# A gated delta-rule recurrence: a chunk's output made by GpSimd, the running products in two parts, the gate's products placed one step later

## What is computed

```python
def step(S, inp):                      # S: 64 x 64 per batch and head, 4 x 16 of them
    qt, kt, vt, at, bt = inp
    err = jnp.einsum('bhij,bhj->bhi', S, kt) - vt
    S = at[..., None] * S - bt[..., None, None] * (err[..., None] * kt[:, :, None, :])
    o = jnp.einsum('bhij,bhj->bhi', S, qt)
    return (S, o)
...
_, o = lax.scan(step, S0, xs)          # 1024 steps
...
mu = o.mean(-1, keepdims=True)
var = ((o - mu) ** 2).mean(-1, keepdims=True)
o = (o - mu) / jnp.sqrt(var + EPS) * ln_w + ln_b
g = jax.nn.sigmoid(x @ Wg.T).reshape(Bb, Tt, H, DV)
o = (o * g).reshape(Bb, Tt, H * DV)
return o @ Wo.T
```

## Time and profile before

| | us |
|---|---|
| median of 3 runs | 4159.57 (4156.91 to 4163.24) |
| the profiled execution's time | 4161.57 |
| its span | 4159.6 |
| DVE busy in the span | 3381.1 (81%) |
| PE busy | 3273.8 (79%) |
| POOL busy | 2340.0 (56%) |
| ACT busy | 2225.8 (54%) |
| L1050 and L1056, 960 instructions each | 723.3 and 723.0 |
| L819, 768 instructions | 552.0 |

### The profile page before, as it was taken

The page is one execution under the profiler, slowest core; times in us unless marked ns, Lnnn a source line. Parts: engine busy times, 40 slices in busy tenths (PEclk is TensorE's granted clock), DMA queues, the critical chain, the costliest instruction groups (busy, mean ns, idle before and its releaser), DMA issues. The chain is left out here.

```text
span 4159.6 us, 113184 instructions
## 1 busy us (share of the span) xinstructions
PE 3273.8 (79%) x45929; PEld 2775.5 (67%) x45929; DVE 3381.1 (81%) x6208; ACT 2225.8 (54%) x5291; POOL 2340.0 (56%) x3045
## 2 busy tenths in 40 slices
PE   5778778777777777777777774377999979988998
PEld 3677777777777777777777774354666647755775
DVE  4599999999999999999999998206888868856885
ACT  3444444444444444444444442324888779936982
POOL 0476776776776767767767766332000058806870
PEclk9888888888888988888888897588999989998999
DMA  2011011011110110110110110410000011101110
GB/s 75 25 39 37 26 42 35 27 46 30 38 39 26 40 37 26 40 37 26 36 35 25 39 32 24 129 39 21 2 2 2 2 31 37 43 8 36 40 37 26
DMA packets 158097, 139.18 MB, mean 33 GB/s; under 512 B 67204, under 2 KB 110416, under 8 KB 157322
## 3 DMA queue, kind: packets, MB, share of 16 engines
q1 hardware_dynamic: 155274, 129.24, 11.3%
q0 software_dynamic: 2304, 2.71, 0.2%
HBM read 96.11 MB, written 16.82 MB: 27 GB/s over the span
## 5 line engine op out<-in xcount | busy, mean ns | idle before, releaser
L1050 DVE TENSOR_TENSOR a_tmp<-a_h,banks 128x128 f32<-128x128 f32 (+14 forms) x960 | 723.3, 753 | 82.6 <-POOL a_h L819 51.6
L1056 DVE TENSOR_REDUCE a_h<-a_tmp 128x64 f32<-128x128 f32 (+14 forms) x960 | 723.0, 753 | 26.4
L819 POOL TENSOR_TENSOR a_h<-a_h,a_a 128x128 f32<-128x128 f32 (+11 forms) x768 | 552.0, 719 | 174.1 <-DVE a_h L1056 162.8
L492 PE MATMUL banks<-a_xseg,a_w_k 128*128 128x128 f32 x2048 | 308.1, 324 | 134.3 <-DVE a_h L1056 130.3
L492 PEld LDWEIGHTS banks<-a_xseg,a_w_k 128*128 128x128 f32 x2048 | 302.1, 239 | 140.8 <-DVE a_h L1056 136.4
L492 PE MATMUL banks<-a_xseg,a_w_v 128*128 128x128 f32 x2048 | 299.1, 318 | 106.2 <-DVE a_h L1056 104.8
L492 PEld LDWEIGHTS banks<-a_xseg,a_w_v 128*128 128x128 f32 x2048 | 293.0, 233 | 111.0 <-DVE a_h L1056 109.5
L804 POOL TENSOR_TENSOR a_st<-a_st,a_ab 128x512 f32<-128x512 f32 x256 | 325.7, 1272 | 0.0
L565 PE MATMUL banks<-a_wm,a_kt 64*64 64x64 f32 x8192 | 257.2, 221 | 84.5 <-ACT a_wm L696 84.5
L565 PEld LDWEIGHTS banks<-a_wm,a_kt 64*64 64x64 f32 x8192 | 248.4, 137 | 95.7 <-ACT a_wm L696 94.0
L696 ACT ACTIVATE a_wm<-a_wt,k_ih_mask 128x256 f32<-128x256 f32 x512 | 211.4, 495 | 164.1 <-DVE a_wt L1070 164.1
(11 more groups left out here) (297 smaller groups left out, 8429.9 us busy)
## 6 DMA issues: line engine op xcount, KB each, us to landing
a_ab<-decays SPq DMA_DIRECT2D x512, 128.0 KB, 3.0
d_Vs<-d_V SPq DMA_DIRECT2D x128, 128.0 KB, 2.3
sent<-k_nothing SPq DMA_DIRECT2D x40, 64.5 KB, 2.3
b_xe<-sent SPq DMA_DIRECT2D x8, 322.5 KB, 3.5
a_xseg<-xn SPq DMA_DIRECT2D x32, 70.0 KB, 3.1
xn<-a_xnT SPq DMA_DIRECT2D x8, 256.0 KB, 2.5
decays<-a_dc SPq DMA_DIRECT2D x128, 8.0 KB
a_xrow<-in_L_attn_x SPq DMA_DIRECT2D x128, 16.0 KB
```

The costliest lines, as they stand in the source:

```text
L492: t = e.matmul(b[:, m * SW:(m + 1) * SW].rearrange("p (b t) -> p b t", b=NB), self.wT[n][:, j, ct * P:(ct + 1) * P], xs[:, :, off:off + SE ...
L819: e.tensor_tensor(self.history(ch, t + 1)[:, :, 0:t], self.history(ch, t)[:, :, 0:t], at, ALU.mult).then_inc(*self.s_hist.at((g, t)))
L1050: e.tensor_tensor(prod, both, gram, ALU.mult).then_inc(*step.at((g, t, "product")))
L1056: e.tensor_reduce(self.results(ch, t), prod, AX.X, ALU.add).then_inc(*step.at((g, t, "w")))
```

## The change

POOL gets pool_output, which makes the chunk's output (the instruction that was L1079 on DVE). In the first chunk it stands at the end of POOL's work for that chunk; in the second it stands inside the running products, which are made in two parts, steps 0 to 5 before it and 6 to 15 behind it. In a first chunk the history product of step 6 is moved ahead of the first gate product, that of step 8 ahead of the second, and that of step 10 ahead of the centring.

```diff
+    def pool_output(self, e, q, s, ch):
+
+        g, c0 = 2 * s + ch, ch * CK
+        q.wait_ge(self.s_pq, g)
+        q.wait_ge(self.s_step, (g, "last", "o"))
+        if s >= 2:
+            q.wait_ge(self.s_turn, s - 2)
+        e.tensor_tensor(self.o2[s % 2][:, c0:c0 + CK, :], self.P2[:, 1], self.O.rearrange("p i t -> p t i"),
+                        ALU.subtract).then_inc(*self.s_o.at(g))
...
-    def pool_cumulate(self, e, q, s):
+    def pool_cumulate(self, e, q, s, j0, j1):
...
-        for j in range(1, CK):
+        for j in range(max(j0, 1), j1):
...
             self.pool_rest(e, q, s, 0)
-            self.pool_history(e, q, s, 0, HAND, 6)
+            self.pool_history(e, q, s, 0, HAND, 7)
             if older >= 0:
                 self.pool_gate(e, q, older, 0)
-            self.pool_history(e, q, s, 0, 6, 8)
+            self.pool_history(e, q, s, 0, 7, 9)
             if older >= 0:
                 self.pool_gate(e, q, older, 1)
-            self.pool_history(e, q, s, 0, 8, 10)
+            self.pool_history(e, q, s, 0, 9, 11)
             if old >= 0:
                 self.pool_centre(e, q, old)
-            self.pool_history(e, q, s, 0, 10, 12)
+            self.pool_history(e, q, s, 0, 11, 12)
...
             self.pool_prepare(e, q, s, 1)
+            self.pool_output(e, q, s, 0)
...
             if more:
-                self.pool_cumulate(e, q, nxt)
+                self.pool_cumulate(e, q, nxt, 0, 6)
+            self.pool_output(e, q, s, 1)
+            if more:
+                self.pool_cumulate(e, q, nxt, 6, CK)
                 self.pool_prepare(e, q, nxt, 0)
...
-        q.wait_ge(self.s_step, (g, "last", "o"))
-        q.wait_ge(self.s_pq, g)
-        if s >= 2:
-            q.wait_ge(self.s_turn, s - 2)
-        e.tensor_tensor(o2[:, c0:row, :], self.P2[:, 1], self.O.rearrange("p i t -> p t i"), ALU.subtract).then_inc(*self.s_o.at(g))
```

More of the change, by code:

```diff
@@ L878, in pool_scale @@
         e.tensor_tensor(o2[:], o2[:], over_i, ALU.mult).then_inc(*self.s_scaled.at(s))
-    def pool_cumulate(self, e, q, s):
+    def pool_cumulate(self, e, q, s, j0, j1):
         view = lambda x, j: x[:].rearrange("p (c t) i -> p c t i", t=CK)[:, :, j, :]
         A, dc = self.a2[s % 2], self.dc[s % 2]
-        q.wait_ge(self.s_a2, s)
-        if s >= 2:
-            q.wait_ge(self.s_pq, 2 * s - 3)
-            q.wait_ge(self.w_decays, (s - 2, 3))
-        e.tensor_copy(view(dc, 0), view(A, 0)).then_inc(*self.s_cum.at((s, 0)))
-        for j in range(1, CK):
+        if j0 == 0:
+            q.wait_ge(self.s_a2, s)
+            if s >= 2:
+                q.wait_ge(self.s_pq, 2 * s - 3)
+                q.wait_ge(self.w_decays, (s - 2, 3))
+            e.tensor_copy(view(dc, 0), view(A, 0)).then_inc(*self.s_cum.at((s, 0)))
+        for j in range(max(j0, 1), j1):
             q.wait_ge(self.s_cum, (s, j - 1))
@@ L912, in gpsimd @@
             self.pool_gram(e, q, 0, n)
-        self.pool_cumulate(e, q, 0)
+        self.pool_cumulate(e, q, 0, 0, CK)
         self.pool_values(e, q, 0)
@@ L1063, in dve_state @@
         g, Wc = 2 * s + ch, self.W[ch]
-        o2, c0, row = self.o2[s % 2], ch * CK, ch * CK + CK
+        c0, row = ch * CK, ch * CK + CK
         more = s + 1 < self.nseg
```

## The result

| | before | changed |
|---|---|---|
| median, us | 4158.24 (4 runs) | 4208.58 (4 runs, 4204.04 to 4211.95) |
| ratio | 1 | 1.0121, 95% interval 1.0103 to 1.0139 |
| span of the profiled execution | 4159.6 | 4202.1 |
| DVE busy in it | 3381.1 | 3326.0 |

The change makes the kernel 50 us slower; the forecast was 4209. DVE has 55 us less to do and the kernel takes longer. The two spans differ by only 42.5 us because the stretch ahead of the recurrence varies from run to run (the first chunk's transpose starts between 159.1 and 170.7 us in the ten traces of this document): from the first to the last of the 64 transposes that end a chunk (L1070, now L1086) it was 2588.1 - 170.7 = 2417.4 us and is 2631.1 - 161.9 = 2469.2, 51.8 us more. This length leaves out what varies outside the recurrence, and the table of experiments gives it for each kernel.

The account below looks back on a forecast made before the run. DVE, busy 92% of a segment, was taken to set the pace. Segment delays of 13 us plus 36 us for PE's clock made 49 us, added to the median 4159.57 for 4209 us; range 4168 to 4232.

Parts of the forecast that it names:

- The output off DVE: Chunk ends on DVE: removing 64 output instructions gains 0, since the last state quarter waits for PE anyway.
- the far end of 68 us: Largest gain from taking the output off DVE, 64 x 1.07 us, if DVE made the last state quarter late.
- The output on POOL: Output takes 1.27 us on POOL: free after first chunks, but makes POOL 1.8 us late after second chunks.
- The long product: POOL's running products at a second chunk's end: one took 1.04 us beside L1079 and should take 0.32.
- DVE late at the segment's start, 1.1 us: Segment start: DVE waits for late POOL and ACT and begins its first step 1.1 us late, 0.7 at L1014 included.
- The gate's product: First chunk of a segment: the 1.73 us wait at step 7 goes; a 1.1 us wait at step 8 comes.
- PE's clock: PE's pause before L516 widens from 1.36 to 3.2 us; slower clock costs 1.2 us a segment, 36 us in all.
- The sum: Whole kernel: 13 us plus 36 us makes it 49 us slower, 4209 us; the forecast proper has chance 0.50.
- The clock holds: Rival at PE's L516: the clock does not fall, or only behind the 64 matmuls; 4173 us, chance 0.17.
- Faster: Rival at step 8: ACT makes up the 1.8 us, sigmoid under 0.7 us late, no wait; 4141 us, chance 0.07.
- Always slow: Rival at PE's k-row matmuls: the slow clock costs 1.9 us in every segment; 4230 us, chance 0.12.
- the lock stays: Rival on POOL: the long product remains or the output is held, POOL 0.7 us later; 4230 us, chance 0.08.

Follow-up runs that it names:

- the first chunk's output alone: The kernel before, with only the first chunk's output made by POOL and the second chunk's still by DVE: 4159.57 us, ratio 0.9989.
- the kernel with the output alone: The changed kernel with the history products back in their old places, output on POOL and running products in two parts: 4259.75 us, ratio 1.0232.
- the kernel with PE kept busy: The changed kernel with PE repeating its second k-row bank's 16 matmuls twice more per segment but the first, in its pause: 4182.76 us, ratio 1.0051.

## Why the prediction was right

- **The output off DVE, 0 us.** Shown. The last quarter's start hasn't moved, and the first chunk's output alone changes 0.1% where 34 us would be 0.8%, and 0.2 us from transpose to transpose. With the far end of 68 us the kernel with the output alone would have been at 4183; it is at 4259.75.
- **The output on POOL.** The first chunk's place is free, as said. In the second chunk the wait of 1.43 us is there (worked out: 1.28). The output's duration was mis-sized: 1.54 us in place of 1.27. L844, from which I took that the stride costs nothing, has its stride in the output, and this operation has it in an input: neither that row nor the 2.08 ns an element could be carried over. So POOL is 2.1 us late in place of 1.8. The factor of two of the Trainium skill, GPSIMD Engine Reference, section 4.1 Engine selection, is not what was measured either: 1.54 to 1.07 is 1.44.
- **The long product.** The 0.7 us that came back with L1079 gone are there: 15 products in 5.91 us in place of 6.62, and none over 336 ns. The prediction gives its start as 1513.4 us; that is the product of 0.32 us ahead of it, the long one started at 1513.8, while L1079 ran. One lock was missed: DVE's L1051 (two inputs in SBUF) took 0.70 us in place of 0.38, because POOL's late Gram product L915 now runs at the same time. It costs nothing of its own, since DVE behind it still waits 0.22 us for ACT.
- **DVE late at the segment's start, 1.1 us.** 1545.66 - 1530.10 = 15.56 us from transpose to first step, before 1524.23 - 1510.15 = 14.08: 1.48 us. It is the term with the output's 0.3 in it. The two new waits of DVE are 0.85 + 0.22 = 1.07 us, as foretold; most of the rest passes under the longer L1051 (0.32 us), behind which ACT still ends last.
- **The gate's product.** The wait at step 7 is gone and one at step 8 has come. Without the clock's part it is 0.99 us (the kernel with PE kept busy), worked out 1.1.
- **PE's clock.** I took 1.2 us a segment between 0 and 1.9; ACT waited 67.4 - 36.7 = 30.7 us more for L516, 1.0 a segment, which is what its rows have over 2.08 us when they are added up (30.9), and the kernel with PE kept busy gave back 29 us. The statement that the fall comes in most segments but not with its whole price in each is what the rows show: 26 of 30 pay something. The whole price was mis-sized: it is 3.68 - 2.08 = 1.60 us, not 1.9. I had doubled the 1.97 us of 32 matmuls at a granted clock of 0.50, which are those of L505, not of L516.
- **The sum.** By the measured terms: start 1.48, step 8 2.01 (60.3 / 30), step 7 -1.72, together 1.77 us, times 30 is 53 us, against 50.3 between the medians and 51.8 inside the recurrence. The forecast's 49 had a start that was 0.4 us short, 11 us in all, and a wait at step 8 that was 0.3 us too long (0.1 in its own part, 0.2 in the clock's), 9 us in all. They cancelled for the most part: that the terms were right to 0.4 us is the working's merit, that the forecast of 4209 is within 1 us is luck.
- **The rivals.** "The clock holds" is what the kernel with PE kept busy makes: 1.0051 of before, 21 us, where I had 13; the difference fits the output's duration (30 x 0.27 = 8 us). "Faster" would have needed the sigmoid less than 0.7 us late; it was late by 2.1 us plus the clock's part. "Always slow" did not come, since only 14 of 30 segments paid the whole price, nor did "the lock stays", since no product is over 336 ns.

## What to carry to other kernels

The engine that is busy 92% of the time need not be the one to relieve: look at what ends the wait just behind the instruction that you would remove. If it is another engine's work that started before it, the instruction is free where it is. On the engine that takes the work over, a wait for the busy engine cost its whole length here (41 of 69 us), since all that stood behind it in that list was late by it; put the moved work behind what others wait for, not among it. And a stretch of idle time that a delay widens on TensorE may cost a second time through its clock.

## What the runs showed of the hardware

- **The clock's second price.** Behind a pause of 1.32 to 1.60 us (the kernel before and the one with PE kept busy) PE's 64 matmuls took 2.08 us in each of the 30 segments from the third on. Behind 1.99 to 2.10 us they took 2.78 to 3.16 in 10 of 30 segments, behind 2.8 us 2.69 to 3.63 in 24 of 30, and behind 3.46 us 2.50 to 3.68 in 26 of 30; in the others they took 2.08. The same pause thus has many prices within one run. I had counted on a spread, not on the same pause going entirely free in four segments.
- **Strides on POOL.** Three operations of two inputs lay on one line of 2.08 ns an element, one of them with a strided output, and L870, strided in its output too, took 1.28 us for 512 elements. The output with a strided input took 1.54 us for 512, 0.27 over the line, and 1.58 with the strides on the two other operands.
- **The lock between DVE and POOL.** DVE's L1079 (both inputs in SBUF) stretched a POOL product that began at 1513.8 us from 0.32 to 1.04 us, until 0.3 us behind the start of DVE's next instruction at 1514.54, and POOL's Gram product stretched DVE's L1051 from 0.38 to 0.70. The state's quarters, with one input in PSUM, ran at 0.69 us beside POOL's products. This is as the Trainium skill, SBUF — State Buffer, section "SBUF: two separate sides", has it: the port pair that VectorE and GpSimd share goes for a whole instruction to whichever of the two starts first, and the other one waits.
